# Gate loops of a graph network: sigmoids to SBUF through two PSUM parts, VectorE's query rows in PSUM

## The reference, cut to what matters

```python
def _gate(h, q, Wg, bg, Wq, bq):            # h: 256 x 768, q: 8 x 64 x 768
    B, L, F = q.shape
    N = h.shape[0] // B                     # 32 nodes per group
    h3 = h.reshape(B, N, F)
    hg = jnp.einsum('bnf,gf->bng', h3, Wg[:, :F])
    qg = jnp.einsum('blf,gf->blg', q, Wg[:, F:]) + bg
    attn = jax.nn.sigmoid(hg[:, :, None, :] + qg[:, None, :, :])
    qi = jnp.einsum('bnlf,blf->bnf', attn, q)
    alpha = jax.nn.sigmoid(jnp.einsum('bnf,gf->bng', h3, Wq[:, :F])
                           + jnp.einsum('bnf,gf->bng', qi, Wq[:, F:]) + bq)
    hn = alpha * jnp.tanh(qi) + (1.0 - alpha) * h3
    return hn.reshape(B * N, F)
```

## Time and profile before

| what | value |
|---|---|
| median of three runs | 1476.81 us (1475.11 to 1479.4) |
| profiled execution, its own time | 1474.77 us |
| its span | 1472.9 us |
| PE busy | 1365.5 us, 93% |
| PE weight loads busy | 1159.6 us, 79% |
| VectorE (DVE) busy | 986.2 us, 67% |
| ScalarE (ACT) busy | 773.5 us, 53% |
| GpSimd (POOL) busy | 207.3 us, 14% |
| chain that ended last, by engine | PE 75%, DVE 13%, ACT 6%, POOL 3% |
| of that, select (L977) and sums (L986) | 6% and 5% |

### The profile page before, as it was taken

The page is one execution under the profiler, slowest core; times in us unless marked ns, Lnnn a source line. Parts: engine busy times, 40 slices in busy tenths (PEclk is TensorE's granted clock), DMA queues, the critical chain, the costliest instruction groups (busy, mean ns, idle before and its releaser), DMA issues.

```text
span 1472.9 us, 24074 instructions
## 1 busy us (share of the span) xinstructions
PE 1365.5 (93%) x10014; PEld 1159.6 (79%) x10014; DVE 986.2 (67%) x1782; ACT 773.5 (53%) x1246; POOL 207.3 (14%) x103
## 2 busy tenths in 40 slices
PE   9999999999999798888798999788999999987998
PEld 8999433899433795687697999777999999976976
DVE  8746777646777657566677677676577677757455
ACT  3446888435888354354544454544355544435433
POOL 0110876000876000102001000000000000000100
PEclk9999999999999999999899999899999999988999
DMA  8456353246363131035243453163454555041100
GB/s 346 118 197 210 92 178 86 71 159 211 100 175 91 65 130 54 0 141 208 81 171 130 149 168 125 28 231 129 133 190 167 193 189 193 34 195 74 54 1 22
DMA packets 30834, 194.81 MB, mean 132 GB/s; under 512 B 4211, under 2 KB 4339, under 8 KB 14726
## 3 DMA queue, kind: packets, MB, share of 16 engines
q1 hardware_dynamic: 30726, 193.27, 38.6%
HBM read 183.03 MB, written 3.93 MB: 127 GB/s over the span
## 4 chain that ended last, share of the span: by engine, by line
PE 75%; DVE 13%; ACT 6%; POOL 3%; issue 1%; DMA 0%; DVEq 0%; SPq 0%; ACTq 0%; POOLq 0%
PE PS L357 59%; PE PS L977 6%; PE PS L986 5%; PE PS L362 3%; DVE WL L300 2%; POOL WK L1172 2%; PE PS L618 1%; PE PS L459 1%; POOL WL L307 1%; DVE SM L534 1%; ACT WH L293 1%; DVE SM L1344 1%; ACT WK L1729 1%; DVE WK L1754 1%; DVE WK L1759 1%
## 5 line engine op out<-in xcount | busy, mean ns | idle before, releaser
L300 DVE TENSOR_TENSOR WL<-w,WH 128x768 fp32r<-128x768 f32 x373 | 355.0, 963 | 211.6 <-ACT WH L293 208.9
L293 ACT ACTIVATE WH<-w 128x768 fp32r<-128x768 f32 x381 | 315.9, 841 | 271.9 <-PE PS L357 258.1
L357 PE MATMUL PS<-XS,WH 128*128 128x256 f32 x2292 | 417.9, 285 | 11.4 <-DVE XS L484 7.1
L357 PEld LDWEIGHTS PS<-XS,WH 128*128 128x128 f32 x2292 | 355.8, 190 | 15.6 <-issue 12.0
L357 PE MATMUL PS<-XS,WL 128*128 128x256 f32 x1146 | 324.0, 283 | 0.0
L357 PEld LDWEIGHTS PS<-XS,WL 128*128 128x128 f32 x1146 | 217.6, 190 | 0.0
L1110 DVE TENSOR_TENSOR WK<-PS,WK 128x1024 f32<-128x1024 f32 x128 | 156.7, 1224 | 55.5 <-ACT PS L1054 54.5
L1172 POOL TENSOR_TENSOR WK<-WK 128x1024 f32<-128x1024 f32 x64 | 152.8, 2390 | 206.0 <-ACT WK L1051 206.0
L357 PE MATMUL PS<-WH,GS 128*128 128x256 f32 x864 | 162.0, 286 | 8.0 <-DVE GS L484 6.5
L1054 ACT ACTIVATE PS<-PS 128x1024 f32<-128x1024 f32 x128 | 129.4, 1011 | 34.4 <-PE PS L977 34.4
L357 PEld LDWEIGHTS PS<-WH,GS 128*128 128x128 f32 x864 | 137.1, 192 | 10.6 <-DVE GS L484 7.4
(11 more groups left out here) (252 smaller groups left out, 2014.3 us busy)
## 6 DMA issues: line engine op xcount, KB each, us to landing
w<-f2W_in SPq DMA_DIRECT2D x40, 1152.0 KB, 5.5
w<-Wrel_in SPq DMA_DIRECT2D x12, 1152.0 KB, 7.8
WK<-qrep_in SPq DMA_DIRECT2D x16, 768.0 KB, 5.5
w<-f1Wi_in SPq DMA_DIRECT2D x8, 1152.0 KB, 6.6
w<-f1Wo_in SPq DMA_DIRECT2D x8, 1152.0 KB, 5.1
w<-f3Wqkv_in SPq DMA_DIRECT2D x6, 1152.0 KB, 13.5
RT<-qg_rows SPq DMA_DIRECT2D x16, 384.0 KB, 6.3
RT<-AS SPq DMA_DIRECT2D x32, 192.0 KB, 6.7
```

The lines of the kernel that those rows point to most:

```text
L293: A.e.activation(w_hi(i), w_raw(i), ACT.Copy).then_inc(*hi("w", i))
L300: V.e.tensor_tensor(w_lo(i), w_raw(i), w_hi(i), ALU.subtract).then_inc(*lo("w", i))
L357: ins = T.e.matmul(o, l, r, start=i == 0 and first, stop=i == n - 1 and last, skip_group_check=lint)
```

## The change

- All three sigmoids write to `SG` in SBUF. The selects write alternately to two PSUM parts (banks 4 and 5, banks 6 and 7): part number 3p + q goes to part (3p + q) mod 2, and a `select` waits for the sigmoid of the part two before it.
- `weigh` multiplies in place in `SG`, by query rows that lie in banks 2 and 3. TensorE writes those once per group (`spread`): two matmuls of 512 columns with 64 rows of `PK` and the group's split query rows `QR` (SBUF, 256 KB per group). `GQ` keeps only GpSimd's 512 columns (256 KB).
- The TensorE order of a pair becomes select 0, select 1, `sums(p-2, 0)`, `sums(p-2, 1)`, select 2, then `spread` for the first pair of a group.
- The split query rows are made once, in the stage ahead: `adj_sync` waits until the `qg` stores have landed, loads `qsel` (1 MB), waits for ScalarE's upper part, issues 8 stores, waits for VectorE's lower part, and issues 8 more; ScalarE's and VectorE's work on them (128 x 2048 each) stands behind `aggregate(2, f)` in `rgcn_act("1")` and `rgcn_vec("1")`.

```diff
@@ adj_sync, at its end
             qg_out.also("qg")
+            L.wait_ge(qg_out, "qg")
+            L.e.dma_start(qsx, dr["qsel"]).then_inc(*qs_in("qs"))
+            for a in range(2):
+                L.wait_ge(*((act, "upper", "qs"), (vec, "lower", "qs"))[a])
+                for g in range(4):
+                    for j in range(2):
+                        L.e.dma_start(qsr[4 * j + g, a, :, :],
+                                      qss[32 * g:32 * g + 32, a, 1024 * j:1024 * (j + 1)].bitcast(F32)).then_inc(*qs_out())
+            qs_out.also("qs")
@@ buffers
-        SP = [PS[:, 1024 * (1 + i):1024 * (2 + i)] for i in range(3)]
+        SP = [PS[:, 1024 * (2 + i):1024 * (3 + i)] for i in range(2)]
+        GP = PS[:, 1024:2048]
-        GQ = [wk(11264 + 1536 * i, n=1536) for i in range(2)]
+        GQ = [wk(11264 + 512 * i, n=512) for i in range(2)]
+        QR = [XS[0:64, 1024 * (1 + i):1024 * (2 + i)] for i in range(2)]
@@ rgcn_act, behind aggregate(2, f)
             if n == "1":
+                A.wait_ge(qs_in, "qs")
+                act_upper(qss[:, 0, :], qsx, "qs")
                 A.wait_ge(pool, "counts")
@@ rgcn_vec, behind aggregate(2, f)
+            if n == "1":
+                vec_lower(qss[:, 1, :], qsx, qss[:, 0, :], "qs")
             vec_gemm(t0, 24, None, 12)
@@ gate_sync: queries(b)
                     o, d = before(b)
-                    for q in range(3):
-                        L.wait_ge(*prod(o, 4 * d + 3, q))
-                L.e.dma_start(GQ[b % 2], dr["qrep"][b]).then_inc(*qin[b % 2](n, b))
+                    L.wait_ge(*prod(o, 4 * d + 3, 1))
+                    L.wait_ge(pe, "gq" + o, d)
+                L.wait_ge(qs_out, "qs")
+                L.e.dma_start(GQ[b % 2], dr["qrep"][b]).then_inc(*qin[b % 2]())
+                L.e.dma_start(QR[b % 2].bitcast(F32), qsr[b].rearrange("a l n -> (a l) n")).then_inc(*qin[b % 2](n, b))
@@ gate_pe: select, spread, and the loop
-                    o = bank_at(2 + 2 * q + i, ("sg" + n, p, q, i),
-                                (act, "sig" + n, p, q) if q == 1 else (vec, "prod" + n, p, q))
+                    o = bank_at(4 + 2 * ((3 * p + q) % 2) + i, ("sg" + n, p, q, i), (act, "sig" + n, p, q))
+            def spread(b):
+                T.wait_ge(qin[b % 2], n, b)
+                for i in range(2):
+                    o = bank_at(2 + i, ("gq" + n, b, i), (vec, "prod" + n, 4 * b + 3, 2))
+                    ins = T.e.matmul(o, PK[0:64, 0:P], QR[b % 2][:, 512 * i:512 * (i + 1)], start=True, stop=True)
+                ins.then_inc(*pe("gq" + n, b))
             gate_q(1)
+            spread(0)
             select(0, 0)
...
                 select(p, 1)
                 sums(p - 2, 0)
+                sums(p - 2, 1)
                 select(p, 2)
-                sums(p - 2, 1)
+                if p % 4 == 0:
+                    spread(p // 4)
@@ gate_act: attend
                 A.wait_ge(pe, "sel" + n, p, q)
+                free_sg(A, n, p)
+                o = SP[(3 * p + q) % 2]
                 if q == 1:
-                    free_sg(A, n, p)
-                    A.e.activation(SG[p % NSG][:, :, 1024:1536], SP[q].rearrange("p (u n) -> p u n", u=2),
+                    A.e.activation(SG[p % NSG][:, :, 1024:1536], o.rearrange("p (u n) -> p u n", u=2),
                                    ACT.Sigmoid).then_inc(*act("sig" + n, p, q))
                 else:
-                    A.e.activation(SP[q], SP[q], ACT.Sigmoid).then_inc(*act("sig" + n, p, q))
+                    A.e.activation(SG[p % NSG][:, q // 2, 0:1024], o, ACT.Sigmoid).then_inc(*act("sig" + n, p, q))
@@ gate_vec: weigh
                 V.wait_ge(act, "sig" + n, p, q)
-                V.wait_ge(qin[p // 4 % 2], n, p // 4)
-                free_sg(V, n, p)
-                V.e.tensor_tensor(SG[p % NSG][:, q // 2, 0:1024], SP[q], GQ[p // 4 % 2][:, 0:1024],
-                                  ALU.mult).then_inc(*vec("prod" + n, p, q))
+                V.wait_ge(pe, "gq" + n, p // 4)
+                g = SG[p % NSG][:, q // 2, 0:1024]
+                V.e.tensor_tensor(g, g, GP, ALU.mult).then_inc(*vec("prod" + n, p, q))
```

More of the change, by code:

```diff
@@ L151, in wait_ge, with build @@
             self.seen[id(sem)] = value
-def build(nc, dr, out, qgr):
+def build(nc, dr, out, qgr, qsr):
     ctx = ExitStack()
@@ L200, in build @@
         pick_in, qg_out = newsem("pick_landed", 16), newsem("qg_stored", 16)
+        qs_in, qs_out = newsem("query_rows_landed", 16), newsem("query_rows_stored", 16)
         gin = [newsem(f"gate_rows_landed{i}", 16) for i in range(2)]
@@ L203, in build @@
         sems = [pe, act, vec, pool, hi, lo, log, *landed, *rowin, x_in, cols_in, edges_in, query_in, lora_in, stored,
-                pick_in, qg_out, *gin, *qin]
+                pick_in, qg_out, qs_in, qs_out, *gin, *qin]
         T, A, V, G, L = Port(pe), Port(act), Port(vec), Port(pool), Port()
@@ L579, in build @@
         qgs = QS[:, :].rearrange("p (a m f) -> p a m f", a=2, m=4)
+        qss, qsx = QS[:, 0:4096].rearrange("p (a n) -> p a n", a=2), wk(4096, n=2048)
         Cr = wk(6144, r=3, m=2, n=256)
@@ L1171, in gate_pool @@
                 G.wait_ge(qin[p // 4 % 2], n, p // 4)
-                G.e.tensor_tensor(s, s, GQ[p // 4 % 2][:, 1024:1536].unsqueeze(1).broadcast_to((P, 2, 512)),
+                G.e.tensor_tensor(s, s, GQ[p // 4 % 2].unsqueeze(1).broadcast_to((P, 2, 512)),
                                   ALU.mult).then_inc(*pool("prod" + n, p, 1))
@@ L2942, in _lay @@
     q = i["L0_gnn_query_embs"].reshape(8, 2, 32, D)
-    a["qrep"] = np.tile(q.transpose(0, 2, 1, 3).reshape(8, 32, 2 * D), (1, 4, 1))
+    q = q.transpose(0, 2, 1, 3).reshape(8, 32, 2 * D)
+    a["qrep"] = np.tile(q[:, :, 1024:], (1, 4, 1))
+    a["qsel"] = q[:, :, :1024].reshape(2, 4, 32, 1024).transpose(1, 2, 0, 3).reshape(P, 2048)
     pick = np.zeros((P, 32, 32), np.float32)
@@ L3035 @@
     qgr = nc.dram_tensor("qg_rows", (8, 2, 32, 2, D), F32, kind="Internal").ap()
-    build(nc, dr, out, qgr)
+    qsr = nc.dram_tensor("query_rows", (8, 2, 32, 1024), F32, kind="Internal").ap()
+    build(nc, dr, out, qgr, qsr)
     r = _run(nc, [{k + "_in": v for k, v in arrays.items()}], core_ids=[0])
```

## The result

The changed kernel takes 1513.05 us (median of 4 runs, 1510.46 to 1515.49) against 1475.96 before; the ratio is 1.0241, 95% interval 1.0209 to 1.0274. The forecast was 1514. The profiled execution takes 1514.87 us, 40.1 more than the one before (1474.77).

The account below looks back on a forecast made before the run. TensorE's own issue was taken as the bound before, a closed chain after. 1474.77 + 29.8 (loops) + 5.5 (hole) + 2.6 (clock) = 1512.7; with 2.0 for the median 1514.7, stated as 1514; 8 in 10 for 1498 to 1529.

Parts of the forecast that it names:

- The bound before: Gate loops of the kernel before: TensorE's own issue sets the period, 3.36 us per pair, 3.44 with transposes.
- The closed chain: Changed gate loops: select 2, its sigmoid, select 1 and both sums set a period of 3.93 us, +14.1 per loop.
- the unseen step: Gate loops, ScalarE's sigmoid end to TensorE's select 1 start: 0.05 us, bounds 0.0 to 0.32.
- What lies beside: Gate loops: transposes and `spread` go free in some 0.7 us of TensorE idle; ScalarE idles 1 us; VectorE's product stays 1.23.
- A whole loop: Each gate loop: 14.1 us from 29 periods plus 0.8 for head and tail; both loops 29.8 us.
- the tail: End of each gate loop: the last part 1 comes later, +0.3 us.
- The stage ahead: Before the loops: rel2 load waits behind query-row stores until 106.95; TensorE hole of 5.5 us, plus 2.6 for the clock.
- The clock: Behind the hole ahead of the loops: granted clock falls to half, 2.6 us lost, bounds 0 and 4.
- The total: Whole kernel: 1512.7 us for the profiled execution, 1514.7 in the runs, stated as 1514.
- Rival A: Gate loops: two parts suffice, TensorE's issue bounds at 3.21 us per pair; 1473 to 1465 us, chance 6%.
- B: Loops as forecast, but rel2 units come in time and the stage ahead is hidden; 1507 us, chance 12%.
- C: Clock falls to half inside the gate loops: period 6.2 us, +130 in both loops, over 1600 us; chance 3%.

Follow-up runs that it names:

- e2: Changed kernel with TensorE's old order, the second sums moved back behind select 2 and `spread`; 1497.6 us, ratio 1.0126 to the kernel before.
- e4: Changed kernel with the sigmoid of part 2 covering 512 of its 1024 columns from pair 3 on; 1493.48 us, ratio 1.0091 to the kernel before.
- e1: Changed kernel with the rel2 weight units loaded right behind `qsel`, ahead of the waits and stores of the split query rows; 1505.02 us, ratio 1.0175.
- e3: Kernel before the change, with only TensorE's order changed: both sums together, then select 2; 1481.05 us, ratio 1.0031.
- e5: Kernel before with grouped sums, all sigmoids to `SG`, in-place products with both VectorE operands in SBUF, three PSUM parts kept; 1573.76 us, ratio 1.0629.
- e8: Kernel of e5 with GpSimd's product covering 512 of its 1024 columns; 1490.62 us, ratio 1.0103 to the kernel before.

## Why the prediction was right

- *The bound before.* TensorE's issue at 3.36: right. Putting select 2 back between the sums restored exactly these starts (e2).
- *The closed chain.* 3.93 forecast, 3.94 measured, and every link is right by itself when it is read from start to start as the forecast read it: select 2 to its sigmoid 0.78 (230.72 to 231.50) for 0.77, the sigmoid 1.03 for 1.02, its end to select 1, the unseen step, 0.05 for 0.05, select 1 to sums 0.66 (232.58 to 233.24) for 0.67, both sums 1.43 (to 234.67) for 1.42. That both the sums and the sigmoid are links is shown by e2 and e4.
- *What lies beside.* `spread` and transposes are hidden in the changed kernel: right, the mean of 3.916 has them inside. For `spread` it was as tight as the forecast's 0.7 us of room for 0.67 says: its pair takes TensorE 3.88 without a wait (e4). ScalarE idles 1.07 (1 forecast); VectorE's product 1.218 (1.23). VectorE waits for `spread` up to 2.39 us once per group, and no one waits for VectorE because of it.
- *A whole loop.* 14.9 forecast, 15.2 measured, of two sizes that were off by about as much either way: the 29 periods gave 13.7 (113.55 less 99.89) for 14.1, since the chain closes only with pair 3 and the first of them took 3.02; what lies outside them gave 1.5 for 0.8, 0.66 of it `spread(0)` and 0.75 the tail, for 0.3.
- *The stage ahead.* 8.1 forecast, 8.6 measured. SyncE's timing was right to 0.2 us (rel2 load at 106.81 for 106.95). The unit landed 6.7 us after issue for 5.8. Why was not tried: the last of the 16 stores in front of it landed at 109.05, and four more weight units were issued behind it from 108.05 on. The product before ended 0.9 us late, for which I had allowed 0.2: VectorE's first subtraction took 1.43 us beside GpSimd's work where the sum had 0.96, and it had taken 1.43 at 100.15 in the trace of before too, a row that the forecast did not use. That delay lies inside the hole and is what e1 keeps. TensorE's late start is 6.3 for 5.5. The clock took 2.3 for 2.6; the 2.6 itself was read a little short, since the earlier trace rows (0.68 in 506 to 507) put the clock's return at 506.6 and not 506.3, which makes 2.8.
- *After the loops* +1.2 that no step had, within what this stretch varies by. Behind loop 2 the profile after has the granted clock at half over TensorE's product at 520, where it was full before at 481.
- *The total.* Part by part the forecast had 37.9 and the profiles differ by 40.1; the medians differ by 37.1, since the profiled run of the changed kernel was 1.8 above its median and that of the kernel before 1.2 below. The parts agree with the profiles to 2.2 us; that 1514 came within 1 us of the median is luck beyond that.
- *Rival A* falls in all its forms: the two parts gate, and even with three (e3) grouping gains nothing. *B* falls, and e1 is what B would have been. *C* falls: the clock is 1.00 in both loops. But the ground given against it, that the clock fell only behind holes of several us, does not hold: in the trace of before it went to half at 708.0 behind three holes of 0.7 to 0.9 us, and in the changed kernel at 519.5 behind holes of 1.2 and 1.4. And where VectorE came late enough, in e5, it did fall inside the loops. C's period adds up to 6.35 by its own terms, not 6.2.

## What to carry to other kernels

Count how many instructions of the producing engine stand between filling a buffer and wanting it again: with two buffers and a burst of three fills, the third waits a whole consumer's latency, and all that is queued behind it waits too. Interleave other work exactly there (e2 gave back 21 of 30 us by moving one line). A new wait in SyncE's program belongs behind every load that has been free until then; ask what the next DMA in that program is, and when its data are wanted.

## What the runs showed of the hardware

- VectorE and GpSimd, both multiplying with all operands in SBUF, cost each other far more than I had expected: VectorE's 1024-column product took 1.21 us at the least and 3.43 at the most (e5), and a median of 1.52 with GpSimd's work halved (e8). With one operand in PSUM it is 1.22 beside the same GpSimd. The Trainium skill (SBUF — State Buffer, Who interferes with whom) says that a VectorE instruction with two SBUF inputs contends with a GpSimd instruction that reads SBUF, and one with at most one SBUF input does not; the runs agree. It is what the query rows in PSUM buy, and it only pays where a product of two SBUF operands would be the alternative.
- A change between 128-column and 32-column stationary operands and back cost some 0.34 us here: the same matmuls of a pair took 3.36 with two such changes and back (before, e2), 3.02 with one (e5).
- Behind a hole of 5.3 us in TensorE's work (110.2 to 115.5) the clock was at half from 113.3 to 120.2, and TensorE worked 4.7 us of that: 2.3 us lost. In e5 holes of 3.3 to 5.0 us, one in most groups, brought the granted clock of both loops down to 0.85 and 0.84.
